# A gated delta-rule attention kernel: all 64x64 products in four corners of the array, state terms ahead of the inverses

## The reference

```python
def step(carry, inp):
    S, R = carry
    kn = k_t / jnp.maximum(jnp.linalg.norm(k_t, axis=-1, keepdims=True), 1e-12)
    pred = jnp.einsum('bhji,bhj->bhi', S, kn)
    r = jnp.clip(v_t - pred, -CLIP, CLIP)
    S = a_t[..., None] * S
    kp = jnp.einsum('bhd,bhde->bhe', kn, S)
    S = S + b_t[..., None, None] * kn[..., None] * (v_t - kp)[..., None, :]
    o = jnp.einsum('bhji,bhj->bhi', S, q_t)
    R = aR_t[..., None] * R
    kpR = jnp.einsum('bhd,bhde->bhe', kn, R)
    R = R + g_t[..., None, None] * kn[..., None] * (r - kpR)[..., None, :]
    o = o + jnp.einsum('bhji,bhj->bhi', R, q_t)
    return ((S, R), o)
```

## Time and profile before

| what | us |
|---|---|
| median of 3 runs (lowest, highest) | 3306.05 (3304.01, 3314.07) |
| the profiled execution, its own time | 3276.76 |
| its span, first to last instruction | 3274.9 |
| TensorE busy (share) | 2773.5 (85%) |
| ScalarE busy (share) | 1943.8 (59%) |
| mean granted TensorE clock, as a share of full | 0.906 |

### The profile page before, as it was taken

The page is one execution under the profiler, slowest core; times in us unless marked ns, Lnnn a source line. Parts: engine busy times, 40 slices in busy tenths (PEclk is TensorE's granted clock), DMA queues, the critical chain, the costliest instruction groups (busy, mean ns, idle before and its releaser), DMA issues. The chain is left out here.

```text
span 3274.9 us, 132532 instructions
## 1 busy us (share of the span) xinstructions
PE 2773.5 (85%) x55642; PEld 2460.6 (75%) x55642; DVE 2721.3 (83%) x6827; ACT 1943.8 (59%) x5180; POOL 953.5 (29%) x928
## 2 busy tenths in 40 slices
PE   3888888888888888888888888888886199999986
PEld 3878888887787888788788888888786177777664
DVE  2889898888989988999999999999997156777776
ACT  2656555556666655666666555666654077666664
POOL 3112222222222222223222222233221101444444
PEclk8988898888888988989999899999998599999998
DMA  3321111111111111111111111111110945777776
GB/s 116 82 64 37 36 35 35 35 35 37 39 35 35 37 37 35 43 35 35 39 40 41 35 35 35 35 42 35 39 40 30 347 144 170 221 217 224 220 217 180
DMA packets 209563, 264.55 MB, mean 81 GB/s; under 512 B 30673, under 2 KB 183250, under 8 KB 208210
## 3 DMA queue, kind: packets, MB, share of 16 engines
q1 hardware_dynamic: 183936, 188.53, 19.0%
q0 software_dynamic: 24576, 67.27, 7.2%
q10 hardware_dynamic: 466, 0.27, 0.0%
HBM read 125.37 MB, written 130.58 MB: 78 GB/s over the span
## 5 line engine op out<-in xcount | busy, mean ns | idle before, releaser
L379 POOL DMA_INDIRECT table<-tail,places x256 | 277.1, 1082 | 721.1 <-DVE BR L852 214.8
L1496 PE MATMUL bank<-w,tail 128*128 x1280 | 357.2, 401 | 31.4 <-ACT tail L1539 14.5
L1468 POOL DMA_INDIRECT tail<-y_table,places x256 | 249.5, 975 | 449.3 <-DMA y_table<-tail 314.0
L1091 POOL COPY inv_r<-N 32x512 f32<-32x512 f32 x128 | 136.4, 1065 | 734.0 <-DVE N L827 730.0
L445 DVE TENSOR_TENSOR tri<-tri,step 128x58 f32<-128x58 f32 (+13 forms) x896 | 305.5, 341 | 30.8
L444 DVE TENSOR_TENSOR step<-tri 128x58 f32<-128x58 f32 (+13 forms) x896 | 301.4, 336 | 26.4
L1496 PEld LDWEIGHTS bank<-w,tail 128*128 128x128 f32 x1280 | 219.2, 191 | 95.9 <-issue 72.7
L1586 DVE TENSOR_TENSOR more<-tail 128x1 f32<-128x1 f32 x320 | 50.8, 159 | 193.7 <-ACT tail L1548 189.6
L1511 PE MATMUL bank<-w,tail 128*128 x640 | 191.1, 380 | 2.7 <-DVE tail L1597 1.4
L1546 ACT ACTIVATE tail<-bank 128x129 f32<-128x129 f32 x320 | 89.8, 281 | 158.9 <-PE bank L1496 156.3
L1482 PE MATMUL bank<-ident,tail 128*128 128x128 f32 x640 | 125.1, 278 | 66.1 <-DMA tail<-table 65.6
(11 more groups left out here) (275 smaller groups left out, 8103.8 us busy)
## 6 DMA issues: line engine op xcount, KB each, us to landing
table<-blank SPq DMA_DIRECT2D x320, 128.5 KB, 3.2
tail<-table SPq DMA_DIRECT2D x320, 128.5 KB
y_table<-tail SPq DMA_DIRECT2D x320, 128.0 KB
w<-in_wpack_dram SPq DMA_DIRECT2D x16, 1540.0 KB, 19.3
tail<-in_x_dram SPq DMA_DIRECT2D x66, 64.0 KB, 2.5
x_rows<-tail SPq DMA_DIRECT2D x32, 128.0 KB
sh_rows<-tail SPq DMA_DIRECT2D x32, 128.0 KB, 1.9
table<-tail,places POOLq DMA_INDIRECT x256, 2.9
```

The lines of the kernel that those rows point to most:

```text
L379: nc.gpsimd.indirect_dma_start(out=table, out_offset=bass.IndirectOffsetOnAxis(ap=t.places[:, TOP * (n - 1) + k:TOP * (n - 1) + k + 1], ax ...
L1468: nc.gpsimd.indirect_dma_start(out=t.term[2 * (m % 2) + k], out_offset=None, in_=d.y_table[0:P * closed(b) + P + 1, :], in_offset=bass.Ind ...
L1496: mm = nc.tensor.matmul(ps[:, 0:257], t.xT_slot[i % 3][:, P * kt:P * kt + P], weights(i, 257 * kt, 257), start=(kt == 0), stop=(kt == 1))
```

## The change

1. **Four corners everywhere.** RQ, KT, SU, RU and PQ are issued like `crossed`. New helpers say which unit a product is (`odd`, `pair`, `mixed`, `out_unit`) and where it then lies (`at_pair`, `at_mixed`, `at_out`). `four` gets the argument `flip`, which swaps the corners of a row, and `rows`. U, B and V are written in the order of the banks; the rows of `wo` on the host follow.
2. **State terms first.** The two terms of O that need only S, R and the queries, and the term of PR that needs only S and the keys, are issued before PE waits for N. Their four banks (`HELD`) are kept until the results are complete: PR's until U is there, O's until W is there. The other jobs rotate over what is left, by an explicit list of free banks.
3. **X of gate 1 behind the prediction.** `second_product(1)` is issued after the second part of PR, and ACT empties it after U (`lower_block(1)`).
4. **Sums ahead of keys.** DVE adds SU into S before the next keys.
5. **ACT** empties the transposed input (XT) before its first layer-norm helper of a chunk.

```diff
+HELD = ("O", "PR")
 def order_of_jobs(n, chunks):
-    jobs += two("Z") + two("X") + two("PR") + two("U") + two("SU") + two("NS") * front + two("O") + [("SD", "")]
-    jobs += two("W") + two("RU") + ends + [("RK", "")] * route + [("OUT", "")] + two("V") * front
+    jobs += two("O") + two("PR") + two("Z") + [("X", "0")] + two("U") + free("PR") + [("X", "1")] + two("SU")
+    jobs += two("NS") * front + [("SD", "")]
+    jobs += two("W") + free("O") + two("RU") + ends + [("RK", "")] * route + [("OUT", "")] + two("V") * front
...
+def pair(i, s):
+    return 4 * (i // 2) + 2 * s + i % 2
+
+def mixed(i, s):
+    return 2 * i + (s ^ i % 2)
...
-                                r, to = slice(C * j, C * j + C), slice(C * (j ^ s), C * (j ^ s) + C)
+                                r, to = slice(C * j, C * j + C), slice(C * (j ^ s ^ flip), C * (j ^ s ^ flip) + C)
...
-                for h in range(2):
-                    units(n, f"RQ{h}", h, [(of(t.kminus[1]), of(t.rqplus))])
+                crossed(n, "RQ", pair, [(of(t.kminus[1]), of(t.rqplus))])
                 for g in range(2):
-                    for h in range(2):
-                        units(n, f"KT{g}{h}", h, [(of(t.kminus[g]), lambda r, u: t.eye[r, :])])
+                    crossed(n, f"KT{g}", pair, [(of(t.kminus[g]), lambda r, u: t.eye[r, :])])
...
+                O, PR = both(n, "O"), both(n, "PR")
+                queries = [(of(t.S), lambda r, u: t.pq[r, 1, u, :]), (of(t.R), of(t.rqplus))]
+                keys = [(lambda r, u: t.pq[r, 0, u, :], of(t.S))]
+                four(O, out_unit, queries, last=False, whole=True, rows=(2, 3, 6, 7), flip=1)[1].then_inc(t.sem["O_flipped"], 1)
+                four(PR, mixed, keys, last=False, whole=True, rows=(1, 3, 5, 7), flip=1)[1].then_inc(t.sem["PR_flipped"], 1)
+                pe.wait_ge(t.sem["O_flipped"], n + 1)
+                four(O, out_unit, queries, first=False, last=False, whole=True, rows=(0, 1, 4, 5))
+                pe.wait_ge(t.sem["PR_flipped"], n + 1)
+                four(PR, mixed, keys, first=False, last=False, whole=True, rows=(0, 2, 4, 6))[1].then_inc(t.sem["O_begun"], 1)
...
                 pe.wait_ge(t.sem["T_ready"], n + 1)
+                second_product(0)
-                PR = [begin(n, "PR0"), begin(n, "PR1")]
-                four(PR, odd_unit, [(lambda r, u: t.pq[r, 0, u, :], of(t.S))], last=False, whole=True)
...
-                for ins in four(PR, odd_unit, [(lambda r, u: t.pqT[r, u, 0, :], of(t.U))], first=False, whole=True):
+                for ins in four(PR, mixed, [(of_pq(0), of(t.U, at_mixed))], first=False, whole=True):
                     ins.then_inc(t.sem["PR_done"], 1)
-                for h in range(2):
-                    units(n, f"SU{h}", h, [(of(t.kT[0]), of(t.U))])
+                second_product(1)
+                crossed(n, "SU", pair, [(of(t.kT[0], at_pair), of(t.U, at_mixed))])
...
                 if route:
                     route_weights(nc, t, link, t.xrow[n % 2])
+                dve.wait_ge(t.sem["O_begun"], n + 1)
+                for h in range(2):
+                    ps = mm(n, f"SU{h}")
+                    nc.vector.tensor_tensor(by_pair(t.S, h), in_pairs(ps), by_pair(t.S, h),
+                                            ALU.add).then_inc(t.sem["dve_emptied"], 1)
...
+                lower_block(0)
                 if front:
                     nc.scalar.activation(tri, t.k[:].rearrange("p u n -> p (u n)"),
                                          ACT.Square).then_inc(t.sem["keys_squared"], 1)
                 for h in range(2):
-                    empty(n, f"U{h}", even_odd(t.U, h))
+                    empty(n, f"U{h}", t.U[:, half[h], :])
+                lower_block(1)
```

More of the change, by code:

```diff
@@ L86, in __init__ @@
         self.engine, self.emptied, self.done, self.before = {}, {}, {}, {}
[L87 to L97 removed]
+        self.place = {}
+        for table, banks in ((SMALL, range(NB)), (WIDE, range(NB, NB + NW))):
+            seen, user = collections.Counter(), {}
+            signalled, ready = 0, collections.deque(banks)
+            for n in range(-1, chunks):
+                for kind, i in order_of_jobs(n, chunks):
+                    if kind == "free" and table is SMALL:
+                        ready.append(self.place[n, i])
+                    if kind not in table:
+                        continue
+                    name, bank = kind + i, ready.popleft()
+                    seen[table[kind]] += 1
+                    signalled += kind not in HELD
+                    self.engine[n, name] = ("" if table is SMALL else "front_", table[kind])
+                    self.done[n, name] = signalled
+                    self.before[n, name] = user.get(bank)
+                    self.emptied[n, name] = seen[table[kind]]
+                    self.place[n, name], user[bank] = bank, (n, name)
+                    if kind not in HELD:
+                        ready.append(bank)
     def bank(self, t, n, name):
[L100 to L101 removed]
+        return t.ps[self.place[n, name]]
     def base(self, name, n):
@@ L536, in begin, with four @@
                 return o.bank(t, n, name)
-            def four(banks, unit, pairs, first=True, last=True, whole=False):
-                for i in range(8):
+            def four(banks, unit, pairs, first=True, last=True, whole=False, rows=range(8), flip=0):
+                for i in rows:
                     for m, (lhsT, rhs) in enumerate(pairs):
@@ L543, in four @@
                         if whole:
-                            begin, end = first and i == 0 and begin, last and i == 7 and end
+                            begin, end = first and i == rows[0] and begin, last and i == rows[-1] and end
                         for s in range(2):
@@ L619, in _ @@
                 need(pe, t, "states_ready", 2 * n - 1)
[L620 removed]
+                crossed(n, "KS", odd, [(of(t.kplus[0]), of(t.S))])
                 if front:
@@ L625, in _ @@
                 need(pe, t, "states_ready", 2 * n)
-                crossed(n, "KR", [(of(t.kplus[1]), of(t.R))])
+                crossed(n, "KR", odd, [(of(t.kplus[1]), of(t.R))])
                 if front:
@@ L1019, in _, with lower_block @@
                 inverse_diagonal(3).then_inc(t.sem["inv_s_ready"], 1)
-                for g in range(2):
+                def lower_block(g):
                     ps = mm(n, f"X{g}")
```

145 lines of the change are left out of this document (65 added, 80 removed).

## The result

The changed kernel takes 3354.79 us (median of 4 runs, 3345.28 to 3357.34) against 3305.03 us (3296.05 to 3314.07) for the kernel before on the same chip: a ratio of 1.0145, 95% interval [1.0111, 1.018]. That is slower by 1.45%, where 3285 us and faster were forecast, and outside the range of 3232 to 3330.

The account below looks back on a forecast made before the run. DVE was taken as the bound; its waits went from 108.7 to 106 us (keys 96, PQ 10), winning 3 us. With part of the 29 us between profile and median, and a little for a faster X1: 3285 us, range 3232 to 3330.

Parts of the forecast that it names:

- what bounds the kernel: Chunk loop: DVE is the bound, its own work unchanged; at most its 108.7 us of waits can be won.
- the mechanism of the added wait: ACT, in order, copies X of gate 1 before the exponentials and norms, so DVE waits 1.6 to 3.5 us a chunk.
- The keys, mis-sized: DVE's wait for ACT's key norms, 43.1 us before: 3.1 us in each of 31 chunks, 96 us.
- rival A: X of gate 1 runs fast: keys' wait falls to 1.6 us a chunk, 3237 us; chance 0.22.
- PQ, counted as unchanged: DVE's wait before PQ is emptied: nothing won, 10 us stays.
- BR, won only in part: DVE's wait for the prediction before BR: all 41.6 us go.
- the spare 0.6 us: Before BR: PR done at 1374.8 at worst, DVE ready at 1375.42, so 0.6 us to spare.
- about 1 us earlier than now: In front of N: PE arrives about 1 us earlier and waits a little longer, worth 0 on DVE's end.
- the 4.4 us that were to be saved in front of N: RQ, KT and PQ in four corners: about 4.4 us less PE work before N; state terms put 3.5 us back.
- Rival B: Clock already low at N, Z products about 2.0 us each: 3342 us, or 3309 and up in part; chance 0.15.
- The conversion to the runs' median: Profiled execution 29 us below the runs' median: if all late-clock chunks, 3274 us; if none, 3303; a little under the middle taken.
- rival C: No change: norms replace BR as DVE's wait, 3.1 to 3.5 us a chunk; 3300 to 3313 us; chance 0.18.

Follow-up runs that it names:

- x1_ahead: The changed kernel with X of gate 1 in front of U again on PE and ACT; ratio 0.9871 to the kernel before.
- xt_back: The changed kernel with ACT's first layer-norm helper ahead of emptying XT again; ratio 1.0064 to the kernel before.
- corners_only: The changed kernel with all moves undone, only the four corners and their layout left; ratio 0.9968 to the kernel before.
- norms_xt_nostate: Changed kernel with NS, SU ahead of X of gate 1, its copies behind the norms, XT order restored, state terms behind N; ratio 0.9975 to before.
- norms_xt_two: Changed kernel with NS, SU ahead of X of gate 1, its copies behind the norms, XT order restored, RQ, KT, SU, RU on two corners; 3227.74 us.
- state_mid: The changed kernel with the state terms of O and PR ahead of the shared expert's products; ratio 1.0116 to the kernel before.

## Why the prediction was wrong, step by step

**Right: what bounds the kernel, and the mechanism of the added wait.** DVE's busy time did not change (2721 and 2718 us), the crossed products take 1.16 us, PE's wait for S before RU and DVE's before the triangles are gone, ACT idles 3.9 us before X of gate 1, and the clock is lower. In the chunk above DVE was ready for the keys 19.2 us behind the start of T (forecast 1382.5 with T of before at 1363.33: 19.2) and the norms came at 22.8 (forecast 20.8 to 22.7). x1_ahead shows that this wait is part 3's.

**The keys, mis-sized: 110 us, not 96.** The term was 31 x 3.1; it measured 31 x 3.55, at the end that the half clock gave for all of the chain, 3.5. The 3.1 left some chunks to a clock that comes back. It came back in none: the granted clock is 0.50 from U to the end of X of gate 1 in all 31 chunks, as the prediction's own argument against rival A said. 14 us.

**PQ, counted as unchanged: 20 and 30 us, not 10.** The sum left out one edit, the order of XT and the layer-norm helper on ACT. The working went through PE and DVE there and not through what ACT's order does to an idle time of PE ahead of a projection. xt_back puts 20 to 30 us of waits and 19 to 26.5 us of the loop on it. This is the step that was missing.

**BR, won only in part: 23 us, not 0.** In the chunk shown PR is done 11.9 us behind the start of T (forecast 10.5 to 11.5) and DVE is ready at 12.0 (forecast 12.1): BR does not wait, but the spare 0.6 us is 0.1. Of the 23 us, 4.3 are the first chunk's, in which DVE has less to do and is ready early, and 14.5 are those of 6 chunks out of 31, all in the last quarter of the loop, in which X of gate 0 starts more than 4 us behind T. For these the failed step is this one: PE reaches N "about 1 us earlier than now", and coming late for N "does not" happen. PE's wait for N in the loop, before and changed:

```profile
PE bank L672 <- DVE N L827: 35.4, 31, 1.4
PE bank L730 <- DVE N L871: 33.3, 25, 2.8
```

It did not grow by 31 us, and in 6 chunks there is none: these are the 6 late ones, in which PE starts Z 0.4 to 2.1 us after N is there. Of the 4.4 us that were to be saved in front of N, RQ and KT gave 2.7, as forecast, PQ 0.35 in the median of the first profile (3.36 us for 3.71) and 1.7 in that of the second (1.98, at full clock), and the slow second projection took 1.6 back in 15 and 23 chunks. The state terms take 3.1. On top of it, PE stands still in the middle of the Z products, and just before them, with nothing that the profile names as releaser:

```profile
2142.27 0.27 PE L601 MATMUL bank<-rqplus,R 64*64 64x64 f32 x2 [1.16 <-issue]
...
2144.03 0.63 PE L730 MATMUL bank<-N,L_r 32*32 32x32 f32 x29
2146.76 1.01 PE L730 MATMUL bank<-N,L_r 32*32 32x32 f32 x30 [2.10 <-issue]
...
2156.88 0.69 DVE L890 TENSOR_TENSOR BR<-V,bank 128x512 f32<-128x512 f32 x1 [2.80 <-PE bank L601]
```

Rival B had a place for a late Z, but by a low clock. These rows show something else, and Z was mostly at half clock in only 3 and 6 of 31 chunks of the two profiles; where PE did wait 4 us for N, in corners_only, rival B's mechanism is there in full.

These three make the sum of waits 153 and 162 us in the two profiles, instead of 106. By the waits the changed kernel should lose 44 us against the profile of before; the loop lost 38.

**The conversion to the runs' median: the step that gave the direction away.** On the profiled execution the sum was 3 us, no change. The forecast of faster came from the 29 us by which the profile of before lies under its runs: I took half of them for chunks with a late clock, which the change would cure. The runs speak against it. A second profile of before has 17 us less in the loop and the same expert tiles, and the medians of before are 3305 us in the first comparison and 3265 to 3272 in all later ones, while the ratio of the changed kernel is the same in both, 1.0145 and 1.0134. What makes the difference between these levels is not in the chunks that the change touches, or the ratio would move. On the first chip it may be the expert part, as in the profile of after; no run of before was profiled at that level, so this is only argued. Without this step the forecast would have been 3303, rival C, and still 50 us short.

**Open.** Why PE stands still in and in front of Z. Most of the stops come where PE has little or no slack in front of N. In before, corners_only and norms_xt_nostate, where PE waits for N in every chunk (35.4, 136.2 and 125.0 us in sum), there is none inside Z; in norms_xt_two, with 3.2 us of such waits, there are 29, from the first chunk on. So "only in the last third" holds for the kernels with some slack, not for that one. state_mid moved the stops from Z into the state terms. This fits instructions that are not yet there when PE does not wait, but no run shows their supply. Why the slack shrinks towards the end of the loop is open, and so is why one profile has 45 us more in the expert part.

## What to carry to other kernels

On an engine that works in order, a copy belongs behind the work that the bound engine waits for, not where its input becomes ready; and the producer must be put in the same order, since moving only the copy won 41 to 49 us of the loop where both won 105 to 113. Parts of a change do not add up: the sums ahead of the keys pay with the state terms ahead of N and brought 90 us of waits in the one kernel that has the sums there but not these, the state terms need the room that the four corners make, and one misplaced part (X of gate 1) hid a gain of 1.3 to 2.2%. Idle time of PE that a saving leaves in front of N is not free either, if the clock falls in it. Cost every reordered line, also one that only fills a gap, and make no term out of the difference between one profile and its runs.

## What the runs showed of the hardware

- One idle of 2.9 us on PE was followed by a clock of 0.53 in a stretch where PE was busy all the time, and the fall came behind the idle, not in it. The order that cut this idle to 0.85 us was worth 0.7%, though it put an idle of over 3 us and the half clock in front of another projection.
- Behind an idle of PE of 4.1 us the 32x32 products ran at half clock (1.92 us for 64 records, corners_only); behind 1.3 us at full clock (1.20, before).
- Sixty-four records in four corners take 1.16 us at full clock and 2.0 at half; on two corners at full clock 2.08 (1.91 for RQ in norms_xt_two). Four corners at half clock are worth no more than two at full.
- X of gate 1 ran at full clock (1.20 us) behind PR and NS, where NS is 3.46 us of 128x128 products; right behind PR it ran at half (1.92). PE was then busy without a gap from 1371.26 to 1377.50 in the changed kernel, all on the lower level.
- The same expert code took 672 us in one profile and 624 to 633 in all the others, with waits on three engines at once that have no releaser.
